# Tenth one-hot table read in every other half and gathered in the others, and all outputs turned to rows for one store

## The reference

```python
e = jnp.stack([tbl_0[ids[:, 0]], tbl_1[ids[:, 1]], ..., tbl_26[ids[:, 26]]], axis=1)   # 2048 x 27 x 128
dot = jnp.einsum('bnd,bmd->bnm', e, e)
z = the pairs i < j of dot                                                            # 2048 x 351
h = jnp.concatenate([z, dense_ctx], axis=1)                                            # 2048 x 367
h = jnp.maximum(h @ W_top1 + b_top1, 0.0)                                              # 512
h = jnp.maximum(h @ W_top2 + b_top2, 0.0)                                              # 256
y = h @ W_top3                                                                         # 2048 x 1
```

## Time and profile before

| | us |
|---|---|
| the three runs | 411.66, 412.40, 415.43 (median 412.4) |
| profiled execution, its time | 412.63 |
| profiled execution, its span (first to last instruction) | 410.5 |

### The profile page before, as it was taken

One profiled execution on the slowest core, in us unless ns is written; L12 is line 12 of the kernel. 1 busy time (PEld: TensorE's weight loads), 2 busy tenths in 40 slices (PEclk: granted clock), 3 DMA queues, 4 the chain that ended last, 5 costly groups with the idle time before them and its releaser, 6 DMA issues.

```text
span 410.5 us, 14146 instructions
## 1 busy us (share of the span) xinstructions
PE 360.7 (88%) x6136; PEld 323.2 (79%) x6136; DVE 264.7 (64%) x799; ACT 166.6 (41%) x229; POOL 260.8 (64%) x280
## 2 busy tenths in 40 slices
PE   1885899999999998999999988999799996989681
PEld 1665888989898888989898978988698986987571
DVE  4998798793869476865689375965549654642200
ACT  3666345543535344343535243244234433354020
POOL 6777777777777777777777777777777775000000
PEclk9999699999999999999999999999789998999997
DMA  7999853443333354334723383344523353000000
GB/s 189 239 251 239 207 122 91 95 91 79 87 84 83 94 65 93 79 93 80 94 71 96 77 56 105 78 93 79 85 71 85 87 69 51 3 2 3 3 0 0
DMA packets 25516, 36.65 MB, mean 89 GB/s; under 512 B 8464, under 2 KB 19728, under 8 KB 25456
## 3 DMA queue, kind: packets, MB, share of 16 engines
q0 software_dynamic: 8704, 17.84, 24.1%
q1 hardware_dynamic: 16752, 17.92, 18.1%
HBM read 35.73 MB, written 0.01 MB: 87 GB/s over the span
## 4 chain that ended last, share of the span: by engine, by line
PE 75%; DMA 7%; issue 7%; ACT 4%; DVE 3%; SPq 2%; ACTq 0%; DVEq 0%
PE embT_ps L320 37%; PE gram_ps L346 13%; PE h_ps L375 11%; PE h_ps L384 7%; DMA embT<-in_tbl 7%; PE embT_ps L330 6%; PE flat_ps L358 2%; ACT embT L499 2%; DVE one_hot L426 1%; ACT pairs L514 1%; DVE flat L455 1%; SPq L254 1%; DVE tbl L407 1%; ACT tbl L483 1%; SPq L247 0%
## 5 line engine op out<-in xcount | busy, mean ns | idle before, releaser
L297 POOL DMA_INDIRECT emb<-in_tbl,idx x272 | 259.9, 956 | 83.8 <-issue 81.1
L426 DVE TENSOR_SCALAR one_hot<-ids,row_of 125x256 fp32r<-125x256 int32 (+1 forms) x688 | 213.8, 384 | 55.5 <-PE embT_ps L320 52.0
L320 PE MATMUL embT_ps<-one_hot,tbl 125*128 125x256 f32 x1376 | 203.7, 300 | 20.7 <-DVE one_hot L426 19.6
L320 PEld LDWEIGHTS embT_ps<-one_hot,tbl 125*128 125x128 f32 x1376 | 182.0, 198 | 33.3 <-issue 14.3
L499 ACT COPY embT<-embT_ps 128x256 f32<-128x256 f32 x80 | 54.6, 682 | 159.3 <-PE embT_ps L320 159.3
L506 ACT COPY embT<-embT_ps 128x512 f32<-128x512 f32 (+1 forms) x80 | 87.9, 1101 | 1.5 <-PE embT_ps L330 1.4
L346 PE MATMUL gram_ps<-embT 128*27 128x27 f32 x4096 | 57.9, 193 | 15.3 <-issue 10.3
L346 PEld LDWEIGHTS gram_ps<-embT 128*27 128x27 f32 x4096 | 47.0, 105 | 30.9 <-issue 22.0
L375 PE MATMUL h_ps<-flatT,w_sb 126*128 126x256 f32 (+1 forms) x216 | 47.4, 374 | 0.0
L330 PE MATMUL embT_ps<-ident,emb 128*128 128x128 f32 x272 | 43.2, 275 | 0.0
L375 PEld LDWEIGHTS h_ps<-flatT,w_sb 126*128 126x128 f32 x216 | 38.0, 201 | 4.2
(11 more groups left out here) (19 smaller groups left out, 34.0 us busy)
## 6 DMA issues: line engine op xcount, KB each, us to landing
ids<-in_ids_hot SPq DMA_DIRECT2D x80, 128.0 KB
emb<-in_tbl,idx POOLq DMA_INDIRECT x272
embT<-in_tbl SPq DMA_DIRECT2D x7, 448.0 KB
embT<-in_tbl SPq DMA_DIRECT2D x3, 560.0 KB
w_sb<-in_W_ring SPq DMA_DIRECT2D x1, 756.0 KB
w_sb<-in_W_top SPq DMA_DIRECT2D x1, 512.0 KB
embT<-in_tbl SPq DMA_DIRECT2D x7, 52.0 KB
out_y<-y_sb SPq DMA_DIRECT2D x16, 0.5 KB
```

Source lines behind the costliest of these rows:

```text
L297: pool.indirect_dma_start(emb[:, t % EB, s, :], None, tables[f][:, :], bass.IndirectOffsetOnAxis(ap=idx[:, t, f:f + 1], axis=0),).then_inc ...
L320: mm = pe.matmul(out[:, 0:HN], tbl[0:ROWS, part, AT[o] + chunk, :], one_hot[0:ROWS, k % SLOTS, c, :], start=(chunk == 0 and part == 0), st ...
L426: done = dve.tensor_scalar(one_hot[0:ROWS, k % SLOTS, c, :], of, row_of[0:ROWS, KINDS.index(CH[o]), chunk:chunk + 1], None, ALU.is_equal)
```

## The change

- **The tenth table** (o = 9, feature 8) is read by one-hot columns only in odd halves (1, 3, 5, 7). In even halves (0, 2, 4, 6) it is gathered as an eighteenth feature, so that the fifth quad of their tiles turns two rows. `feature_order` puts feature 8 behind the seventeen gathered ones, `slot(o)` gives its place in `embT`, `emb` has 18 places, and the waits count the rows landed.
- **Order of reads**: in the even halves 2, 4, 6 the nine reads are split four to five, and the first quad of the odd tile has no read behind it.
- **Ids of half 0**: ACT subtracts the first row number of each partition (`relative_ids`, with a bias operand), and DVE compares with a constant rather than with `row_of`.
- **End**: layer 1 of tile 14 moves into tile 15, ahead of the last quad, and layer 2 of tile 14 ahead of the ring and flat of 15.
- **Store**: the sixteen stores go. At the very end TensorE turns `y_sb` (128 x 16) into 16 rows of 128, DVE copies them from PSUM, and SP stores 16 rows of 512 bytes in one transfer.

```diff
-    return [f for f in range(feats) if f not in ONE_HOT] + list(ONE_HOT)
+    return [f for f in range(feats) if f not in ONE_HOT] + [ONE_HOT[-1], *ONE_HOT[:-1]]
...
+    def hots_of(h):
+        return range(O if h % 2 else O - 1)
+    def slot(o):
+        return GF if o == O - 1 else GF + 1 + o
+    def quad(t, q):
+        return range(q * QUAD, min(FEATS - len(hots_of(t // HT)), (q + 1) * QUAD))
...
-            hots = [("hot", h, o) for o in (range(O // 2) if odd else range(O // 2, O))]
+            both = hots_of(h)
+            hots = [("hot", h, o) for o in (both[:len(both) // 2] if odd else both[len(both) // 2:])]
...
-            after[3] += [("layer2", t - 3), ("ring", t - 1), ("flat", t - 1), ("layer2", t - 2)]
+            after[QUADS - 2] += [("layer2", t - 3), ("ring", t - 1), ("flat", t - 1), ("layer2", t - 2),
+                                 ("layer1", t - 1)]
...
-    END = [("dots", T - 1, 0, GROUPS32), ("layer1", T - 2), ("ring", T - 1), ("flat", T - 1), ("layer2", T - 2),
-           ("layer1", T - 1), ("layer2", T - 1)]
+    END = [("dots", T - 1, 0, GROUPS32), ("layer2", T - 2), ("ring", T - 1), ("flat", T - 1), ("layer1", T - 1),
+           ("layer2", T - 1)]
...
-        def store(sp, t):
-            sp.wait_ge(y_ready, t + 1)
-            sp.dma_start(y[t * TILE:(t + 1) * TILE, :], y_sb[:, t:t + 1]).then_inc(y_stored, 16)
...
-            sp.wait_ge(y_stored, 16 * T)
+            sp.wait_ge(y_in_rows, 1)
+            sp.dma_start(y.rearrange("(t c) o -> t (c o)", c=TILE), h2[0:T, 0:TILE]).then_inc(y_stored, 16)
+            sp.wait_ge(y_stored, 16)
...
+            pe.wait_ge(y_ready, T)
+            pe.transpose(flat_ps[0:T, 0:TILE], y_sb[:, :], ident[:, :]).then_inc(y_turned, 1)
...
+                        if n < len(HOT0):
+                            done = dve.tensor_scalar(columns, of.bitcast(F32), float(chunk), None, ALU.is_equal)
...
+            dve.wait_ge(y_turned, 1)
+            dve.tensor_copy(h2[0:T, 0:TILE], flat_ps[0:T, 0:TILE]).then_inc(y_in_rows, 1)
...
-                act.copy(ids[0:ROWS, n % IDS, :].bitcast(F32), ids[0:ROWS, n % IDS, :]).then_inc(ids_as_floats, 1)
+                act.activation(ids[0:ROWS, n % IDS, :].bitcast(F32), ids[0:ROWS, n % IDS, :], ACT.Identity,
+                               bias=minus_row[0:ROWS, kind:kind + 1]).then_inc(ids_relative, 1)
```

More of the change, by code:

```diff
@@ L53, in dlrm_tower @@
     assert D == P and FEATS == 2 * HALF + 1 and KC * PER_CHUNK == FEATS and KR == PER_CHUNK * (HALF + 1)
-    GATHERED = [f for f in range(FEATS) if f not in ONE_HOT]
-    GF = len(GATHERED)
     O = len(ONE_HOT)
+    GATHERED = feature_order(FEATS)[:FEATS - O + 1]
+    GF = FEATS - O
     QUAD = 4
     QUADS = -(-GF // QUAD)
+    assert GF % QUAD
     EB = 2
@@ L84, in dlrm_tower, with rows_landed @@
     RAWS = HT * TILE * PITCH // RAW
-    def quad(q):
-        return range(q * QUAD, min(GF, (q + 1) * QUAD))
+    def hots_of(h):
[4 more added lines that the diff above has]
+        return range(q * QUAD, min(FEATS - len(hots_of(t // HT)), (q + 1) * QUAD))
+    def rows_landed(t, q):
+        return sum(len(quad(s, q)) for s in range(t % EB, t + 1, EB))
     def plan(t):
@@ L139, in dlrm_tower @@
     READ = {step: n for n, step in enumerate(HOTS)}
+    FIRST = [min(h for _, h, q in HOTS if q == o) for o in range(O)]
     ctx = ExitStack()
@@ L266, in _ @@
             sp.dma_start(b2_sb[:, :], b2.to_broadcast([P, H2])).then_inc(weights_loaded, 16)
-            stored = 0
-            for n in range(O, len(HOTS)):
-                while HT * HOTS[n][1] - 1 >= stored + 7:
-                    store(sp, stored)
-                    stored += 1
+            for n in range(len(HOT0), len(HOTS)):
                 load_ids(n)
-            for t in range(stored, T):
-                store(sp, t)
-            sp.wait_ge(y_stored, 16 * T)
+            sp.wait_ge(y_in_rows, 1)
+            sp.dma_start(y.rearrange("(t c) o -> t (c o)", c=TILE), h2[0:T, 0:TILE]).then_inc(y_stored, 16)
+            sp.wait_ge(y_stored, 16)
         @block.gpsimd
@@ L294, in _ @@
                         pool.wait_ge(turned, TURNED["quad", t - EB, q])
-                    for s in quad(q):
+                    for s in quad(t, q):
                         f = GATHERED[s]
@@ L464, in _ @@
             dve.wait_ge(rows_ready, len(KINDS))
+            for i in range(len(KINDS)):
+                dve.tensor_scalar(minus_row[:, i:i + 1], row_of[:, i, 0:1], -1.0, None, ALU.mult).then_inc(rows_ready, 1)
             for o in range(O):
                 split_low(o)
-                build(o)
+                if o < len(HOT0):
+                    build(o)
             for kind, *of in ORDER:
-                if kind == "hot" and READ["hot", of[0], of[1]] + LOOK >= O:
+                if kind == "hot" and READ["hot", of[0], of[1]] + LOOK >= len(HOT0):
                     n = READ["hot", of[0], of[1]] + LOOK
@@ L498, in copy_hot @@
                 at = h % 2 * HT
-                act.copy(embT_feats[:, at:at + HT, GF + o, :],
+                act.copy(embT_feats[:, at:at + HT, slot(o), :],
                          embT_ps[USE["hot", h, o] % BANKS][:, 0:HN].rearrange("p (t c) -> p t c", t=HT),
@@ L503, in copy_quad @@
             def copy_quad(t, q):
-                n = len(quad(q))
+                s = quad(t, q)
+                n = len(s)
                 act.wait_ge(turned, TURNED["quad", t, q])
-                act.copy(embT_feats[:, t % TB, quad(q)[0]:quad(q)[0] + n, :],
+                act.copy(embT_feats[:, t % TB, s[0]:s[0] + n, :],
                          embT_ps[USE["quad", t, q] % BANKS][:, 0:n * P].rearrange("p (f c) -> p f c", f=n),
@@ L533, in _ @@
             split_high(0)
-            float_ids(0)
+            relative_ids(0)
             for kind, *of in ORDER:
```

40 lines of the change are left out of this document (24 added, 16 removed).

## The result

| | before | changed kernel |
|---|---|---|
| median, us | 412.9 (4 runs, 411.66 to 415.43) | 387.28 (4 runs, 386.11 to 388.28) |
| profiled execution: time, span | 412.63, 410.5 | 386.11, 384.1 |

What follows compares the result with a forecast made beforehand. TensorE was taken as the bound in the middle, transfers at the start, a chain of single steps at the end. From 412.63 us, +0.6 start, -7.1 reads, -0.7 last steps, -4.1 store gave 401.3 us; range 396.5 to 406.

Steps and rivals of the forecast that it cites:

- The sixteen stores in the middle sat on SP's queue alone ... nothing.: Middle: removing the stores gains nothing, since they preceded only id loads that DVE waited for just once there.
- The burst stays as long, so I keep the stall: Dots of tile 15: TensorE runs out of instructions in a burst of 512, so the 3.43 us stall remains.
- the stall goes because the instructions stand elsewhere: Rival, dots of tile 15: shifted instruction packets remove the stall, 397.5 us; chance 0.13.
- The reads in halves 2, 4, 6: -7.1: Middle, TensorE: three table reads of 2.6 us go, 0.7 us of turns is added, net -7.1 us.
- waits take the place of the reads: Rival, middle: waits for banks, flat chain or compares lose half of the 7.1 us, 404.9 us; chance 0.11.
- The gathers ... more than 20 us of cover. Nothing.: POOL: eight more gathers, last start 354.5, needed at 378 for quad 4 of tile 15; costs nothing.
- the gathers become the bound: Rival, POOL: issues so slowly that quad 4 of tile 15 comes near 395, giving 418 us; chance 0.03.
- The start: +0.6, between -0.7 and +1.4: Up to half 1: ids let it begin 0.7 us earlier, low clock after idling costs 1.3; +0.6 in all.
- The last steps: -0.7: New order in tiles 14 and 15: dots start 3.2 us later, 4.2 us less behind them; -0.7 taken.
- The +1.1 for a low clock: Last steps: layer 2 of tile 14, behind the stall, may run at low clock, costing up to 1.1 us.
- The store: -4.1: End: SP's wait falls from 7.0 to 2.3 us, turn and copy add 0.6; -4.1 us.
- lands no sooner: Rival, end: the store's receipt is slow whatever the pieces, 406.0 us; chance 0.13.

Runs made afterwards that it cites:

- Experiment 1: Kernel before with only the new store: none in the middle, outputs turned to rows, one transfer of 16 pieces of 512 bytes; 388.75 us, ratio 0.956.
- experiment 4: Changed kernel with the sixteen old stores put back and nothing else undone; 407.24 us, ratio 1.003.
- experiment 2: Kernel before with its sixteen stores of 4-byte pieces all issued at the very end; 402.18 us, ratio 0.989.
- experiment 7: Changed kernel with the old order of the last steps (layer 1 of tile 14 after the dots of tile 15); 387.46 us, ratio 0.959.
- experiment 3: Kernel before with sixteen stores at the old places, each one piece of 512 bytes of other values; 387.96 us, ratio 0.954.
- experiment 6: Changed kernel with the ids of the first two reads of half 1 loaded ahead of dense inputs and weights; 387.16 us, ratio 0.958.
- experiment 5: Changed kernel measured again, nothing altered; 388.11 us, ratio 0.961.
- experiment 11: Kernel before with each of its sixteen stores cut to 16 pieces of 4 bytes; 389.36 us, ratio 0.960.
- 12: Kernel before with each of its sixteen stores writing 8 pieces of 64 bytes of other values; 384.24 us, ratio 0.947.

## Why the prediction was wrong, step by step

**"The sixteen stores in the middle sat on SP's queue alone ... nothing."** This is the step that failed. The prediction looked for who waits *on SP's queue* behind a store, found nobody, and stopped. Experiment 1 puts the cost at 16.6 us of the middle against the profiled execution of the kernel before, experiment 4 at 11.8 in the changed kernel (269.5 against 257.6). Up to the end of layer 3 experiment 2 has 18.5 us by the traces and 11.5 by the times of one chip. Each of these is more than the whole sum of 11.3. The signs stood in the trace of before and weren't summed: two dips of the clock in the middle and one at the end, nine stalls of 10.3 us in the dots. The mechanism, as far as the traces go: transfers take longer (0.182 against 0.141 us for a packet of a gather), the fetch of instructions among them. Transfers while the dots of tile 15 run, of the kernel before (383.5 to 387 us), the changed one (366 to 371) and experiment 1 (366 to 368):

```profile
q8 instruction: 1, 0.02, 5.3%
```

```profile
q8 instruction: 1, 0.02, 1.2%
```

```profile
q8 instruction: 1, 0.02, 2.9%
```

One packet took 3.0 us before (0.053 x 16 x 3.5), and 1.0 and 0.9 us in the others. (Of the two packets of the earlier trace rows only this one ran beside the dots.) In the middle the packet is late rather than long. Transfers of the kernel before, 288 to 294 us:

```profile
q8 instruction: 1, 0.02, 1.0%
```

That is 0.96 us, but the packet does not move before 291.8, and TensorE has stood since 289.9. The work behind a stop may run at 1.2 GHz: the 3.76 us for the read at 294.52.

A second sign is where TensorE stops. Count each matmul with its weight load as a pair, over the whole program: the longest stall in the dots of tile 15 stands behind pair 6003 or 6004 in twelve of the fourteen profiles, though these dots begin anywhere from pair 5765 to 5819. In experiment 7 it stands behind 5877, some 127 pairs earlier, and experiment 4 has stalls behind 5876, 5895 and 6004. So the place hangs on the position in the list of instructions, as it would with a fetch.

The steps up to "small pieces in number make stalls" are shown by experiments; that the late fetch is the link between them is read from these few packets and places, and no run here isolates it.

**"The burst stays as long, so I keep the stall" (3.43 us).** Half right. A stall stays in every kernel, and is 2.0 to 2.4 us long wherever no store of 128 pieces stands in the middle. Its length was a matter of the stores: 3.43 to 1.99, -1.4 in the changed kernel. The rival "the stall goes because the instructions stand elsewhere" is refuted: the stall moved with them (from 190 pairs into the dots to 239, and to 136 in experiment 7) and did not go, and in experiment 3, where they stand where they stood, it is 2.35 us.

**The reads in halves 2, 4, 6: -7.1.** Measured -4.9 for the middle (experiment 1 against the changed kernel). A tile pair takes 43.8 us with ten reads. In the changed kernel the three tiles that have four reads rather than five take 20.0, 20.3 and 19.7 us rather than 21.7 to 21.8, so the whole gain lies there, and it is 1.8 of the 2.6. The other 0.8 us went where the rival "waits take the place of the reads" looked for it; the traces don't settle by which engine.

**"The gathers ... more than 20 us of cover. Nothing."** Wrong in size. The count was right (last start predicted at 354.5, measured 355.6), but the cover was made of the stalls. With them gone quad 4 of tile 15 comes at 365.8 rather than at the forecast 378, and quad 3 at 357.2, which is when its rows land. So POOL is now as much the bound as TensorE, and experiment 6 shows it: 9.4 us gained at the start return as 8.6 us of waits for gathers. The rival "the gathers become the bound" had the right engine, but was priced for a POOL that gets slower, not for a TensorE that gets faster.

**The start: +0.6, between -0.7 and +1.4.** Measured +2.3 to +2.7. The wait was seen (DVE behind the ids, TensorE idle, low clock behind it), but the ids came 1.6 us later rather than 0.6 earlier, and TensorE idled 8.5 us rather than 4.4. Over all runs the dots of tile 2 stand at 84.8 to 89.6, mean 87.0, in kernels with the old start and at 88.4 to 90.5, mean 89.8, in those with the new one (the latter with experiment 7): +2.8. Why the ids come later stays open. In the end the loss cost nothing, since the gathers would have taken it anyway (experiment 6).

**The last steps: -0.7.** Against experiment 1 the trace has -0.6 (34.7 to 34.1). Each term came about as worked out: the dots 3.05 us later behind layer 2 of tile 13 (forecast 3.2), 4.2 us less behind them (4.2). The +1.1 for a low clock was met in the profile of experiment 5 and not in the first. Experiment 7 shows that the times don't tell the two orders apart.

**The store: -4.1.** The mechanism was right: the pieces were what was slow. It was under-sized: SP waits 1.0 us, where 2.3 had been taken from the load of 13.5 KB. With turn and copy at 0.7 us (forecast 0.6) the end is 5.4 us shorter. The rival "lands no sooner" is refuted, by experiments 3, 11 and 12 too (0.8 to 1.0 us). The new store takes 1.4 us from issue to landing. The fixed cost of about 2.0 us that the Trainium skill (DMA: Bandwidth & Descriptors, "Anatomy of one DMA") gives, in a section on DMAs that GpSimd issues, is above that and far under the 7.0 of the old store, which SP issued. The remark of the same page (Specifications) that less than 512 B is read, modified and written speaks against small pieces as such, and experiment 11 had sixteen of 4 bytes in 1.0 us.

**In one line.** Of some 26 us in the span, the store brought 16.6 (middle) + 1.3 (last steps) + 5.3 (behind layer 3) = 23.2, and all the rest of the change 4.9 - 2.7 + 0.6 = 2.8. These are single executions; by the times on one chip the store is worth 17.8 us, and of the rest they show nothing: changed kernel 387.3 and 388.1, the kernel before without small stores 388.75, 387.96, 389.36 and 384.24; and the rest of the change alone, with the old stores, 1.003.

## What to carry to other kernels

A transfer that nobody waits for is not free: sum up the idle times with the releaser "issue", the dips of the granted clock and the time of a packet on the other queues, and look what was issued some microseconds ahead of them. Store results as rows (one turn on TensorE and one copy, 0.7 us here) rather than as a column of 4 bytes from each of 128 partitions, also in the middle of a kernel. When a stall goes, work out again which engine is next: the cover of every other step was measured with the stall in it. And keep a trace of the kernel before from each chip: the one trace here, of a long execution, gave 18.5 us up to the end of layer 3 where the times of one chip leave 11.5.

## What the runs showed of the hardware

- A store of 128 pieces of 4 bytes was waited for 7.0 to 7.4 us at the end. One of 16 x 4 bytes took 1.0, of 8 x 64 bytes 0.9, of 1 x 512 bytes 0.8, and of 16 x 512 bytes 1.0 us. That 16 pieces are harmless and 128 are not was unexpected; where between them it turns wasn't tried.
- With such stores in the middle, a packet of the gathers takes 0.182 to 0.200 us in the mean rather than 0.141; some 4 to 9 us behind a pair of them it takes 1.04 us (240 to 245 us of the kernel before), and 0.14 with none near. Sixteen of them, 8 KB in all, cost the middle 16.6 us in one execution of the old reads and 11.8 in one of the new. When all sixteen stood behind the last gather, a packet took 0.140 us (experiment 2: 19.1% of the span for 8704 packets).
- A burst of 256 weight loads and 256 short matmuls stalled TensorE in every profile, for 2.0 us at least, 130 to 239 pairs in; in twelve of fourteen profiles behind the same pair of the program, 6003 or 6004, and in experiment 7 some 127 pairs ahead of it.
- A compare of 256 columns on VectorE took 0.32 us with the number from a tensor and 0.23 us with a constant.
